# Low-rank part of a fused attention and feed-forward kernel: xa computed twice over, B's two products in the two row halves of the array

## The reference, cut to what matters

```python
x = x + _layernorm(attn(_layernorm(x), Wq, bq, Wk, bk, Wv, bv, Wo, bo))
x = x + _layernorm(ffn(_layernorm(x), kernel, bias, a, b))

def ffn(x, kernel, bias, a, b):          # x: [16, 4096, 1024]
    w = simulate_quantize_int4(kernel)   # [1024, 1024]
    y = jnp.einsum('bsd,df->bsf', x, w) + bias
    lora = jnp.einsum('bsr,rf->bsf', jnp.einsum('bsd,dr->bsr', x, a), b)   # rank 16
    return y + lora
```

## Time and profile before

| | us |
|---|---|
| median of 3 runs | 1731.31 (1729.13 to 1731.7) |
| profiled execution | 1730.8 |
| its span, slowest of the cores | 1729.2 |
| spans of the 8 cores | 1722.3 to 1729.2 |

### The profile page before, as it was taken

How to read it: one execution, slowest core, us unless ns; L and a number is a source line. 1 busy time by engine, 2 the same in 40 slices (tenths; PEclk the granted TensorE clock), 3 DMA queues, 4 the chain that set the end, 5 groups by cost and what they waited for, 6 DMA issues and landing times.

```text
span 1729.2 us, 27326 instructions; the slowest of 8 cores (1722.3 to 1729.2 us)
## 1 busy us (share of the span) xinstructions
PE 1688.0 (98%) x8388; PEld 777.9 (45%) x8555; DVE 975.9 (56%) x1771; ACT 659.1 (38%) x859; POOL 316.2 (18%) x950
## 2 busy tenths in 40 slices
PE   6999999999999999999999999999999999999997
PEld 2544444444444444444444444444444444444443
DVE  3766775555413455545555666675656655554554
ACT  3543333333213333334343344344443343442451
POOL 0331111111000111111212222222222221111111
PEclk9999999999999999999999999999999999999998
DMA  9989989855222334744454465677555444443441
GB/s 288 279 216 273 263 223 242 229 148 150 72 90 50 69 106 105 167 109 104 132 137 123 120 178 130 188 216 205 158 139 115 121 116 117 114 111 89 97 117 54
DMA packets 347810, 257.62 MB, mean 149 GB/s; under 512 B 272209, under 2 KB 305361, under 8 KB 343570
## 3 DMA queue, kind: packets, MB, share of 16 engines
q1 hardware_dynamic: 301298, 177.52, 43.0%
q10 hardware_dynamic: 46368, 78.34, 13.8%
HBM read 122.63 MB, written 67.11 MB: 110 GB/s over the span
## 4 chain that ended last, share of the span: by engine, by line
PE 91%; DMA 2%; issue 2%; SPq 2%; DVE 1%; ACT 1%; POOL 1%; ACTq 0%; DVEq 0%; POOLq 0%
PE O L568 25%; PE S L546 25%; PE F L598 12%; PE S L467 12%; PE F L503 6%; PE O L503 5%; PE F L602 2%; DMA hT<-h 1%; DMA wst<-wk 1%; SPq L1152 1%; PE F L568 1%; PE X L581 1%; PE O L489 1%; PE F L359 0%; PE F L489 0%
## 5 line engine op out<-in xcount | busy, mean ns | idle before, releaser
L546 PE MATMUL S<-hT,Gq 128*128 128x512 bf16 (+3 forms) x2203 | 450.5, 360 | 2.0
L568 PE MATMUL O<-V,PT 128*128 128x512 bf16 x2013 | 449.8, 379 | 1.9
L1020 ACT ACTIVATE SA<-S,cq 128x512 f32<-128x512 f32 (+3 forms) x288 | 186.3, 651 | 537.2 <-PE S L546 513.5
L546 PEld LDWEIGHTS S<-hT,Gq 128*128 128x128 bf16 x2240 | 215.2, 98 | 237.6
L568 PEld LDWEIGHTS O<-V,PT 128*128 128x128 bf16 x2048 | 200.2, 98 | 242.0 <-issue 0.8
L467 PE MATMUL S<-hT,M 128*128 128x512 bf16 x1002 | 229.3, 379 | 3.6 <-ACT Gst L991 2.5
L598 PE MATMUL F<-W,h2T 128*128 128x512 bf16 x950 | 220.6, 382 | 5.4 <-issue 4.1
L803 DVE TENSOR_REDUCE st<-SA 128x1 f32<-128x512 f32 (+3 forms) x288 | 174.5, 633 | 65.4 <-ACT SA L1020 58.4
L1029 ACT ACTIVATE P<-SA,st 128x1280 bf16<-128x1280 f32 (+13 forms) x104 | 142.5, 1371 | 57.6 <-DVE st L812 54.2
L467 PEld LDWEIGHTS S<-hT,M 128*128 128x128 bf16 x1024 | 99.9, 98 | 122.3 <-issue 3.2
L967 ACT ACTIVATE h<-xr,stA 128x1024 bf16<-128x1024 f32 x56 | 69.5, 1241 | 221.6 <-DVE junk L738 194.6
(11 more groups left out here) (141 smaller groups left out, 1324.5 us busy)
## 6 DMA issues: line engine op xcount, KB each, us to landing
xr<-x SPq DMA_DIRECT2D x124, 512.0 KB, 4.6
y<-xr ACTq DMA_DIRECT2D x63, 512.0 KB, 2.7
Gq<-g_scr SPq DMA_DIRECT2D x63, 256.0 KB, 3.1
g_scr<-Gst ACTq DMA_DIRECT2D x60, 256.0 KB, 3.5
h_scr<-hT SPq DMA_DIRECT2D x8, 1024.0 KB, 8.7
v_scr<-V ACTq DMA_DIRECT2D x8, 1024.0 KB, 7.9
hT<-h_scr ACTq DMA_DIRECT2D x8, 1024.0 KB, 5.1
V<-v_scr ACTq DMA_DIRECT2D x8, 1024.0 KB, 7.4
```

The source lines that it names most:

```text
L546: mm = t.matmul(out=SR[(j + 2) % 3][:, 0:wd], lhsT=gq(i)[:, dc * 128:(dc + 1) * 128], rhs=hT[:, sl * 4096 + dc * 512:sl * 4096 + dc * 512 ...
L568: mm = t.matmul(out=values_pair(i)[:, hh * 512:(hh + 1) * 512], lhsT=PT[:, (i % 2) * 4096 + blk * 128:(i % 2) * 4096 + (blk + 1) * 128], r ...
L1020: s.activation(out=SA[:, c * 512:c * 512 + wd], in_=SR[(j + 2) % 3][:, 0:wd], func=AF.Abs, bias=cq[:, seq * 32 + tile:seq * 32 + tile + 1] ...
```

## The change

XA has sixteen products instead of eight, in four rounds over the four column groups. Groups 0 and 2 sum the even tiles, groups 1 and 3 the odd ones; so partitions 0 to 63 of `X0` together hold the whole sum, and partitions 64 to 127 hold it once more. B's product for the first half of the columns takes partitions 0 to 63 of `xaT` and `B4`, with the tile position (0, 0), and that for the second half partitions 64 to 127, at (64, 0). The bias row and the 1 that takes it up now stand at partitions 16 and 80, with one small DMA more.

```diff
-    one16_h = nc.inline_tensor((np.arange(128)[:, None] == 16).astype(np.float32), "one16_h").ap()
+    one16_h = nc.inline_tensor((np.arange(128)[:, None] % 64 == 16).astype(np.float32), "one16_h").ap()
...
-            for dc in range(8):
-                q = 32 * (dc % 4)
-                mm = t.matmul(out=X0[q:q + 32, 0:128], lhsT=a_bf[:, dc * 32:(dc + 1) * 32],
-                              rhs=h2T[:, o + dc * 128:o + (dc + 1) * 128], start=(dc < 4), stop=(dc >= 4),
-                              tile_position=(0, q))
+            for r in range(4):
+                for j in range(4):
+                    dc = 2 * r + j % 2
+                    mm = t.matmul(out=X0[32 * j:32 * j + 32, 0:128], lhsT=a_bf[:, dc * 32:(dc + 1) * 32],
+                                  rhs=h2T[:, o + dc * 128:o + (dc + 1) * 128], start=(r == 0), stop=(r == 3),
+                                  tile_position=(0, 32 * j))
             mm.then_inc(xp_d, 1)
...
-                    mm = t.matmul(out=ffn_bank(i, hh), lhsT=xaT[:, (i % 2) * 128:(i % 2 + 1) * 128],
-                                  rhs=B4[:, hh * 512:(hh + 1) * 512], start=False, stop=True)
+                    mm = t.matmul(out=ffn_bank(i, hh), lhsT=xaT[64 * hh:64 * hh + 64, (i % 2) * 128:(i % 2 + 1) * 128],
+                                  rhs=B4[64 * hh:64 * hh + 64, hh * 512:(hh + 1) * 512], start=False, stop=True,
+                                  tile_position=(64 * hh, 0))
...
-                v.wait_ge(fb_ld, 80)
+                v.wait_ge(fb_ld, 96)
...
-                sp.dma_start(out=fbst[16:17, :], in_=fbias_h).then_inc(fb_ld, 16)
+                for q in (16, 80):
+                    sp.dma_start(out=fbst[q:q + 1, :], in_=fbias_h).then_inc(fb_ld, 16)
```

## The result

The changed kernel takes 1738.58 us (median of 20 runs) against 1730.83 us before (20 runs): ratio 1.0038, 95% interval 1.0031 to 1.0046. It is slower by 0.4%, +6.6 us on 1731.

A forecast was written before the change was run, and what follows sets the result against it. TensorE was taken to bound the loop; XA's added rounds 7.2 us, B 0.3 - 0.2 + 0.33 and the slow XA 0.1 summed to +7.7, on the median 1731.31 giving 1739.0 us, range 1731 to 1748.

The forecast's parts named there:

- the forecast's own case: B's halves overlap, going in and out costs what XA pays: 1736 to 1744 us, chance 0.56.
- TensorE is the path: In the loop over row blocks, a microsecond more of TensorE is a microsecond more of span; other engines have slack.
- the 0.11: XA's two added rounds cost TensorE 0.11 us in each of 64 blocks, +7.2 us.
- the switch ahead of B: Changing tile shape around B's pair between full-array products: 0.22 us in and out together.
- XA, 2 x 0.056: Each of XA's two added rounds costs 0.056 us, the spacing of full-array 128x128 matmuls.
- the upper end of 0.07: Upper bound for each added XA round, from the spacing of the existing two rounds: +9.0 us in all.
- B, +0.005 a block: B's pair: in and out 0.22 plus streaming 0.216, together 0.44 against 0.43; +0.3 us over 61 blocks.
- The weight load: B's loads of 64 rows keep the fast load, 0.098 us; 0 added, though 0.08 more was possible.
- rival 3: Switch paid and B's weight load slow, 0.08 to 0.16 us more: 1744 to 1749 us, chance 0.13.
- the loop's sum: XA's added rounds and B's +0.005 together, over the 61 blocks running W, B, values: +7.1 us.
- The tail, +0.2: Last blocks: -0.2 where XA directly follows B twice, +0.33 for the last block's separate halves, +0.1 for slow XA.
- Rivals 1, 2 and 4: 1: no switch paid, 1725.2, chance 0.11; 2: switch 0.08 to 0.17, chance 0.12; 4: halves don't overlap, 1752, chance 0.08.

The follow-up runs named there:

- XA alone: Kernel before with XA's products doubled to sixteen, B still over all 128 rows; ratio 1.0027 in its second run.
- the one-half kernel: Changed kernel with both of B's products in the same row half, so nothing can overlap; ratio 1.0121 against the kernel before.
- the kernel with 40 blocks: Kernel before with W, B and values in row halves and VectorE adding X0's halves, in 40 picked blocks only; ratio 1.0015.

## Why the prediction was right

1739.0 us were predicted, +0.44%; +0.38% was measured, and the forecast's own case came true in sign, mechanism and size. That 1739.0 is so near the median of 1738.58 is in part luck: the ratio puts the change at +6.6 us where the sum had +7.7. Point by point:

- TensorE is the path: it held in the loop except where B waits. I had said that the 0.11 is lost where B waits, in three places, and had still summed it over all 64 blocks. The cover does more than that. In five blocks (the 2nd, 8th, 12th, 16th and 51st) the doubled XA costs nothing, as TensorE waits for VectorE anyway: 5 x 0.11 = 0.56 us less. In three of them the switch ahead of B also lies within the wait and only the overlap is left: the change gains 0.2 each, 0.6 less.
- XA, 2 x 0.056: right. The two added rounds are 112 ns together by XA alone; the upper end of 0.07 is out.
- B, +0.005 a block: -0.003. The overlap is whole (0.212 by the one-half kernel), in and out cost 0.21 rather than 0.22.
- The weight load costs no more than before: B's loads are 0.093 each, started together, where they were 0.098. So rival 3 is out. The Trainium skill's rule that the prediction names ("TensorE: Matmul & The Clock Gate", section "Weight-path perf modes"), by which the fast load asks only for 128 weights of a type other than FP32, agrees with that.
- So the loop's sum was 61 x 0.117 = +7.1 and came out at 56 x 0.109 - 0.6 = +5.5. What was mis-sized is the number of blocks in which XA counts (56 and not 61, 0.6), the 8 ns by which B's pair is cheaper (0.5), and the overlap gained under three waits, which I had left out (0.6). What the whole run shows beyond that (+6.6, interval 5.4 to 8.0) isn't more than its spread.
- The tail, +0.2: as a whole not told apart. From the 62nd XA to the last B's start it is 15.6 to 18.4 us before, by core, and 17.4 to 17.6 after, since the clock falls at another point there. Its pieces can be read where the clock is full. Where XA stands directly behind B, from the last W matmul to XA is 0.63 instead of 0.74, the 0.1 gained. But I counted two such places, and there is one: in the second XA comes 3.5 us behind B, as it waits for the transfer of h2T, which the earlier trace rows had shown. In the last block the way into B and out of it costs 0.1 each time, as forecast.
- L515 was the row that decided, against L511: a product of 64 rows pays the switch, in every experiment that has one between full-array products. L515 names no tile position, and B's halves have both, a position and 64 rows; which of the two counts there wasn't separated, nor why L511 pays nothing. Rivals 1, 2 and 4 are out by the changed kernel's B rows, 0.39 long, 0.31 behind the last W matmul and 0.32 ahead of the values product.

## What to carry to other kernels

A pair of small-tile products that saves one streaming of 512 columns and stands alone between full-array products earns nothing here: in and out of the shape cost as much as it saves. The gain was there only where the neighbours already have the shape, or where the way in lies under a wait. On a path that is nearly all TensorE, compare the length of a loop from one instruction's first start to its last over all cores: it told 0.1 us from nothing where whole runs told 2.

## What the runs showed of the hardware

- A change of tile shape costs 0.09 to 0.10 us in which the array stands idle and some 0.01 of a load that is no longer hidden, each way, at the full clock, for four column groups, two row halves or one row half alike; for one row (L515) 0.09 on the way in. From row halves straight to column groups, in the tail, it is 0.10 once.
- Two row halves keep the full rate over whole blocks of W and values, with twice as many weight loads: 0.108 us for each half product.
- A wait of TensorE of 2.4 us was followed by half the clock on five of eight cores and not on three, in the same execution, and one of 2.0 us in the kernel with 40 blocks on three of eight; it then cost 1.7 us more. Behind the one of 1.7 us in the kernel before, no core's clock fell.
